# An attention scorer on one core: the last 24 steps in three blocks of eight, and VectorE's share of their weighted sums as halving adds in SBUF

## The chip, the core and the metric

The kernel runs on one core of a Trainium2 chip. The metric is the device time of one execution in microseconds (us). Before the change three runs gave 293.14, 293.26 and 296.01 us; the median is 293.26 us.

## What is computed

For each of B = 512 rows there is a sequence of S = 200 vectors of D = 64 numbers, a target vector and a mask. A small network (256 to 80 to 40 to 1 units, sigmoids between) scores every step against the target. A masked softmax over the 200 scores gives weights, and the output is the weighted sum of the sequence.

```python
tgt = concat([tgt, pos], -1) @ proj_w + proj_b
din = concat([tgt, seq, tgt - seq, tgt * seq], -1)
h = sigmoid(din @ w1 + b1)
h = sigmoid(h @ w2 + b2)
score = (h @ w3 + b3)[..., 0]
score = where(mask == 0, -1e9, score)
attn = softmax(score, -1)
out = einsum('bs,bsd->bd', attn, seq)
```

Everything is fp32.

## The kernel before

The 512 rows lie on 128 partitions, four to a partition (q = 0 to 3). The program is one loop over groups of eight steps (25 groups, index g), and each engine has its own instruction list, written out by hand and tied together with semaphores. Within a group VectorE (DVE in the profile) transposes the sequence (L541), multiplies it with the target (L550) and adds the target's part to the first layer's result (L676, L683). TensorE (PE) does the three layers (L389, L399; L415, L422; L435), and ScalarE (ACT) the nonlinearities (L277, L286, L293).

The stages of a group are shifted against each other: in turn n of the loop, layer 1 works on group n, layer 2 on n - 1, layer 3 on n - 2 and the transposition of the scores and the softmax step on n - 3. There are 25 turns with new groups and three more (n = 25, 26, 27) that only drain.

Layer 3 and what follows it work by blocks of 16 steps: 12 blocks of 16 and a last one of 8, indices c = 0 to 12. After the last group of a block TensorE runs `layer3(c)`, ScalarE copies the scores out (`rows`, L305), TensorE transposes them (L445), and VectorE does `softmax_step(c)`: masked copy, running maximum, subtraction (L659 to L670). ScalarE takes the exponentials (L319). The block's share of the output is then accumulated online: `acc = acc * exp(old max - new max) + sum over steps of e * seq`, with one more column for the sum of the weights.

GpSimd (POOL) does this sum. It multiplies the block with the exponentials into `mix` (L508), copies the exponentials into the extra column (L511), scales `acc` (L512) and halves `mix` by adds until one step is left (L519), then adds it to `acc` (L523). For the last three blocks (`SHARED` = 10, 11, 12) it does only the first rows of each partition (`KEPT` = 2, 1, 1 of the four); VectorE does the others in `share_sum`. VectorE's way differs from GpSimd's: ScalarE writes its exponentials a second time into a PSUM bank (L316, `exp_v`), the product is written with the steps innermost (L637), and one TENSOR_REDUCE (L644) sums it into PSUM (`part_v`); L640 and L646 scale and add to `acc`. `share_sum(10)` stands in turn 25, `share_sum(11)` and `share_sum(12)` behind the loop.

The blocks of the sequence that the sums read are loaded into a ring of two buffers (`seq_sb`, SyncE's queue, L241 and L248). The load of a block waits until the block two before it has been read. Masked scores and shifted scores have two buffers each, the exponentials `E` three.

Of the kernel before, what the change touches and what calls it, by code (L numbers as in the profile page):

```python
# [5 lines left out]
def din_attention_program(nc, r_mask, seq, target, pos_emb, proj_w, proj_b, w1, b1, w2, b2, w3, b3, out):  # L6
# [15 lines left out]
    P = 128  # L22
# [5 lines left out]
    NBLK = -(-S // BLK)  # L28
# [22 lines left out]
    def last_pair(c):  # L51
        return (c * BLK + steps_of(c)) // 2 - 1

    def block_of_last_group(g):
        c = g * 8 // BLK
        return c if 0 <= g < NGRP and 4 * g + 3 == last_pair(c) else None
# [13 lines left out]
    with ctx:  # L70
# [11 lines left out]
        seq_sb = [sb(f"seq_sb{r}", [P, Q, BLK, D]) for r in range(RING)]  # L82
# [52 lines left out]
        mix_v = sb("mix_v", [P, MOST * D * BLK])  # L135
# [12 lines left out]
        s_seq = [sem(f"seq_loaded{r}") for r in range(RING)]  # L148
# [34 lines left out]
        s_exp_v = sem("exp_for_vector_done")  # L183
# [10 lines left out]


        shared_bank = {SHARED: pT, SHARED + 1: pB, SHARED + 2: pL2[0]}

        def exp_v(c):
            w, k = steps_of(c) + 1, Q - KEPT[c]
            return shared_bank[c][:, 0:k * w].rearrange("p (q x) -> p q x", q=k)  # L200

        def part_v(c):
            k = Q - KEPT[c]
            return shared_bank[c][:, 256:256 + k * (D + 1)].rearrange("p (q d) -> p q d", q=k)
# [9 lines left out]
        def _(sp):  # L214
# [527 lines left out]
```

## Time and profile before

| | |
|---|---|
| median of 3 runs | 293.26 us |
| the profiled execution | 293.81 us |
| its span | 292.0 us |
| PE busy | 250.3 us, 86% |
| DVE busy | 235.7 us, 81% |
| POOL busy | 193.7 us, 66% |
| ACT busy | 154.7 us, 53% |
| TensorE's granted clock, mean | 0.972 |

The span runs from the first to the last instruction of the profiled execution; 1.8 us of its time lie around the span. Busy shares are means over the whole span. The loop's body and the drain at its end have different limits, so the end is read by itself, in the timeline.

### The profile page before, as it was taken

How to read it: one execution, taken by the hardware profiler on the slowest of the kernel's cores; microseconds unless marked ns; L12 is line 12 of the kernel's file. 1: busy time of each engine (PE TensorE's matmuls, PEld its weight loads, DVE VectorE, ACT ScalarE, POOL GpSimd, SP SyncE). 2: the span in 40 equal slices, each digit the busy share in tenths (PEclk: the TensorE clock that was granted, in tenths of full speed). 3: DMA queues.
4: the chain of work that ended last, by engine and by line, in shares of the span. 5: the costliest groups of instructions: out<-in, count | busy, mean ns of one | idle time of the engine just before them, and what ended most of it. 6: DMA issues, size and time to landing. Idle time of an engine off the chain costs nothing.

```text
span 292.0 us, 5476 instructions
## 1 busy us (share of the span) xinstructions
PE 250.3 (86%) x2084; PEld 77.9 (27%) x2084; DVE 235.7 (81%) x331; ACT 154.7 (53%) x257; POOL 193.7 (66%) x125
## 2 busy tenths in 40 slices
PE   4659999999999999999999999999999999998100
PEld 2213323222322232323223323322233223222000
DVE  3598999689687886896887868968968799549696
ACT  2003467665666476556755674666566647656100
POOL 2000000009979979979799799797997997987970
PEclk9999999999999999999999999999999999999855
DMA  6989999999799999999999999899898860431200
GB/s 117 167 125 175 162 176 261 214 165 309 126 202 284 179 329 145 161 326 162 270 214 176 323 171 272 201 154 319 130 178 304 133 270 0 136 153 29 114 0 18
DMA packets 216749, 53.68 MB, mean 184 GB/s; under 512 B 209556, under 2 KB 210068, under 8 KB 216724
## 3 DMA queue, kind: packets, MB, share of 16 engines
q1 hardware_dynamic: 211640, 52.70, 82.3%
q10 hardware_dynamic: 5084, 0.64, 1.4%
q8 instruction: 16, 0.26, 0.4%
q14 instruction: 9, 0.07, 0.1%
HBM read 53.20 MB, written 0.13 MB: 183 GB/s over the span
## 4 chain that ended last, share of the span: by engine, by line
DVE 47%; PE 33%; issue 11%; POOL 3%; SPq 2%; DMA 1%; ACT 1%; DVEq 0%; ACTq 0%; POOLq 0%
DVE X L550 15%; PE pA L389 12%; DVE X L541 11%; DVE HidA L676 10%; PE pB L399 8%; PE pA L435 7%; DVE mix_v L637 3%; DVE HidB L683 2%; PE pA L445 2%; PE pL L415 2%; POOL mix L519 2%; POOL mix L508 1%; DVE pB L644 1%; PE pL L422 1%; DMA proj_b<-in_L_rec_proj_b 1%
## 5 line engine op out<-in xcount | busy, mean ns | idle before, releaser
L519 POOL TENSOR_TENSOR mix<-mix 128x260 f32<-128x260 f32 (+5 forms) x51 | 96.9, 1900 | 5.2 <-POOL acc L512 0.5
L277 ACT ACTIVATE HidA<-HidA,VA 128x512 f32<-128x512 f32 x100 | 66.8, 719 | 52.7 <-DVE HidA L676 52.7
L286 ACT ACTIVATE G<-pL,bias 128x512 f32<-128x512 f32 x100 | 60.5, 688 | 47.0 <-PE pL L422 47.0
L508 POOL TENSOR_TENSOR mix<-seq_sb,E 128x4096 f32<-128x4096 f32 (+3 forms) x13 | 77.2, 5941 | 0.4 <-POOL acc L523 0.3
L550 DVE SCALAR_TENSOR_TENSOR X<-pT,P_pair,X 128x512 f32<-128x512 f32 x100 | 69.8, 739 | 0.2
L676 DVE TENSOR_TENSOR HidA<-pA,UA 128x1024 f32<-128x1024 f32 x50 | 59.8, 1196 | 4.6 <-PE pA L389 4.2
L541 DVE STREAM_TRANSPOSE X<-squares 128x1024 f32<-128x1024 f32 x50 | 61.7, 1235 | 0.0
L389 PE MATMUL pA<-X,w_seq 64*64 64x512 f32 x400 | 55.0, 621 | 4.3 <-DVE HidA L676 3.7
L506 POOL MEMSET masked<- 128x64 f32 x11 | 1.7, 152 | 82.5 <-ACT E L319 82.5
L389 PE MATMUL pA<-X,w_sb 64*64 64x512 f32 x400 | 53.7, 608 | 0.0
L399 PE MATMUL pB<-X,wB 128*32 128x512 f32 x400 | 47.8, 596 | 0.0
L415 PE MATMUL pL<-HidA,w2A 64*64 64x512 f32 x400 | 47.6, 590 | 0.0
L683 DVE TENSOR_TENSOR HidB<-pB,UB 128x512 f32<-128x512 f32 x25 | 17.2, 687 | 28.5 <-PE pB L399 28.5
L422 PE MATMUL pL<-HidB,w2B 32*128 32x512 f32 x200 | 28.5, 640 | 0.0
L435 PE MATMUL pA<-G,w3s 128*32 128x512 f32 x200 | 24.1, 599 | 4.8 <-DVE HidA L676 4.8
L389 PEld LDWEIGHTS pA<-X,w_sb 64*64 64x64 f32 x400 | 15.7, 137 | 28.9 <-issue 28.9
L389 PEld LDWEIGHTS pA<-X,w_seq 64*64 64x64 f32 x400 | 12.2, 134 | 40.2 <-issue 26.1
L415 PEld LDWEIGHTS pL<-HidA,w2A 64*64 64x64 f32 x400 | 15.1, 133 | 28.2 <-issue 26.0
L293 ACT ACTIVATE HidB<-HidB,VB 128x512 f32<-128x512 f32 x25 | 18.1, 723 | 7.7 <-DVE HidB L683 7.3
L399 PEld LDWEIGHTS pB<-X,wB 128*32 128x32 f32 x400 | 11.6, 109 | 24.9 <-issue 24.9
L445 PE MATMUL pA<-ident,rows 128*128 128x128 f32 x52 | 8.5, 285 | 6.7 <-DVE HidA L676 4.5
L422 PEld LDWEIGHTS pL<-HidB,w2B 32*128 32x128 f32 x200 | 7.8, 182 | 20.3 <-issue 19.5
(96 smaller groups left out, 106.1 us busy)
## 6 DMA issues: line engine op xcount, KB each, us to landing
squares<-in_L_rec_sequence_emb SPq DMA_DIRECT2D x98, 256.0 KB, 4.7
seq_sb<-in_L_rec_sequence_emb SPq DMA_DIRECT2D x12, 2048.0 KB, 9.9
seq_sb<-in_L_rec_sequence_emb SPq DMA_DIRECT2D x1, 1024.0 KB, 5.1
squares<-in_L_rec_sequence_emb ACTq DMA_DIRECT2D x2, 256.0 KB, 6.1
mask_i<-in_r_mask SPq DMA_DIRECT2D x1, 400.0 KB, 5.5
tgt_sb<-in_L_rec_target_emb SPq DMA_DIRECT2D x1, 128.0 KB, 2.2
out_dram<-result SPq DMA_DIRECT2D x1, 128.0 KB, 2.0
w_sb<-in_L_rec_w ACTq DMA_DIRECT2D x1, 80.0 KB, 3.8
```

The source lines that it names most:

```text
L277: last = nc.scalar.activation(h, h, ACT.Tanh, scale=0.5, bias=VA[:, 4 * u + i:4 * u + i + 1])
L286: nc.scalar.activation(G[p % NG][:, :], pL2[p % 4][:, :], ACT.Tanh, scale=0.5, bias=bias2[:, 0:1])\
L389: last = nc.tensor.matmul(pA[k * HALF:(k + 1) * HALF, i * 512:(i + 1) * 512], w[half, :], x(2 * u + k)[half, :], start=(x is x1), stop=(x ...
L399: last = nc.tensor.matmul(pB[32 * j:32 * j + 32, :], wB_2d(n), x(4 * g + j), start=(n == 0), stop=(n == 1))
L415: nc.tensor.matmul(pL2[2 * k + r][i * HALF:(i + 1) * HALF, :], w2A[half, :], HidA[u % NZA][half, i, :], start=True, stop=False)
L422: last = nc.tensor.matmul(pL2[j][:, :], w2B[quarter, :, :].rearrange("k a m -> k (a m)"), HidB[g % NZB][quarter, :], start=False, stop=True)
L435: last = nc.tensor.matmul(pL3[j * TILE:(j + 1) * TILE, :], w3s[:, k, :], G[p % NG][:, :], start=(k == 0), stop=(k == per - 1))
L508: nc.gpsimd.tensor_tensor(mix[:, 0:k, 0:n, 0:D], seq_sb[c % RING][:, 0:k, 0:n, :], e[:, 0:k, 1:n + 1].unsqueeze(3).to_broadcast([P, k, n, ...
L519: nc.gpsimd.tensor_tensor(mix[:, 0:k, 0:n, :], mix[:, 0:k, 0:n, :], mix[:, 0:k, n:2 * n, :], ALU.add)\
L541: nc.vector.transpose(X1[g % 2][:, 2 * k:2 * k + 2, :], squares[g % SQRING][:, :, 2 * k:2 * k + 2, :].rearrange("p k m d -> p m k d"))\
L550: nc.vector.scalar_tensor_tensor(out=X2[p % NX][:, :], in0=pT[:, :], scalar=P_pair[:, p:p + 1], in1=X1[p // 4 % 2][:, p % 4, :], op0=ALU.a ...
L676: nc.vector.tensor_tensor(HidA[u % NZA][:, :, :], pA[:, :].rearrange("p (i b) -> p i b", i=2), UA[:, :].unsqueeze(1).to_broadcast([P, 2, 5 ...
```

## The change

Blocks are cut anew: 11 blocks of 16 steps and three of 8 (`NFULL` = 11, `SHORT` = 3), c = 0 to 13. Block 10 (steps 160 to 175) stays as it was; steps 176 to 199, which were a block of 16 and one of 8, are blocks 11, 12 and 13. The shared blocks are now 10 to 13, with 2, 1, 1 and 1 rows kept by GpSimd. Each short block has its own `layer3`, `rows`, transposition and softmax step, one turn of the loop after the other (24 to 27), and `share_sum(c)` stands one turn behind the softmax step of c, ahead of that of c + 1.

`share_sum` takes GpSimd's form: the product with the features innermost, a copy of the exponentials into a 65th column, halving adds in `mix_v`, then scaling and adding to `acc`. It reads the exponentials from the same SBUF buffer `E` as GpSimd, and ScalarE writes them once. PSUM has no part in it any longer. Blocks 12 and 13 have sequence buffers of their own, so that their loads wait for nothing; `masked` and `E` have four buffers; two set-up tensors are placed in buffers of `G`.

```diff
-    NBLK = -(-S // BLK)
+    SHORT = 3
+    NFULL = (S - SHORT * 8) // BLK
+    NBLK = NFULL + SHORT
...
-    SHARED = NBLK - 3
-    KEPT = {SHARED: 2, SHARED + 1: 1, SHARED + 2: 1}
+    SHARED = NBLK - 4
+    KEPT = {SHARED: 2, SHARED + 1: 1, SHARED + 2: 1, SHARED + 3: 1}
...
+    def first_step(c):
+        return min(c, NFULL) * BLK + max(c - NFULL, 0) * 8
...
+        def ring(c):
+            return c % RING if c < NBLK - 2 else c - (NBLK - 2) + RING
...
             for c in range((NGRP - 2 - 5) // 2 + 1, NBLK):
-                sp.wait_ge(s_mix, c - RING + 1)
-                if c - RING >= SHARED:
-                    sp.wait_ge(s_part, PART * (c - RING - SHARED) + 1)
+                if c < NBLK - 2:
+                    sp.wait_ge(s_mix, c - RING + 1)
...
                     w = steps_of(c) + 1
-                    k = KEPT.get(c, Q)
-                    if k < Q:
-                        if c == SHARED + 1:
-                            act.wait_ge(s_zb, NGRP)
-                        nc.scalar.activation(exp_v(c), shifted[c % 2][:, k:Q, 0:w], ACT.Exp).then_inc(s_exp_v, 1)
                     if c >= NE:
                         act.wait_ge(s_sum, c - NE + 1)
-                    nc.scalar.activation(E[c % NE][:, 0:k, 0:w], shifted[c % 2][:, 0:k, 0:w], ACT.Exp).then_inc(s_exp, 1)
+                    nc.scalar.activation(E[c % NE][:, :, 0:w], shifted[c % 2][:, :, 0:w], ACT.Exp).then_inc(s_exp, 1)
...
                 n, q0 = steps_of(c), KEPT[c]
                 k = Q - q0
-                done = PART * (c - SHARED)
-                e, part = exp_v(c), part_v(c)
-                prod = mix_v[:, 0:k * D * n].rearrange("p (q d s) -> p q d s", q=k, d=D)
-                dve.wait_ge(s_exp_v, c - SHARED + 1)
-                dve.wait_ge(s_seq[c % RING], 16 * (c // RING + 1))
-                dve.wait_ge(s_sum, SHARED if c == SHARED or KEPT[c - 1] == q0 and c > SHARED + 1 else c)
+                done = parts(c)
+                e = E[c % NE]
+                prod = mix_v[:, 0:k * n * (D + 1)].rearrange("p (q s d) -> p q s d", q=k, s=n)
+                dve.wait_ge(s_exp, c + 1)
+                dve.wait_ge(s_seq[ring(c)], seq_count(c))
                 if done:
                     dve.wait_ge(s_part, done)
-                nc.vector.tensor_tensor(prod.rearrange("p q d s -> p q s d"), seq_sb[c % RING][:, q0:Q, 0:n, :],
-                                        e[:, :, 1:n + 1].unsqueeze(3).to_broadcast([P, k, n, D]), ALU.mult)\
+                nc.vector.tensor_tensor(prod[:, :, :, 0:D], seq_of(c)[:, q0:Q, 0:n, :],
+                                        e[:, q0:Q, 1:n + 1].unsqueeze(3).to_broadcast([P, k, n, D]), ALU.mult)\
                   .then_inc(s_part, 1)
-                nc.vector.tensor_tensor(acc[:, q0:Q, :], acc[:, q0:Q, :], e[:, :, 0:1].to_broadcast([P, k, D + 1]),
+                nc.vector.tensor_copy(prod[:, :, :, D], e[:, q0:Q, 1:n + 1]).then_inc(s_part, 1)
+                done += 2
+                while n > 1:
+                    n //= 2
+                    dve.wait_ge(s_part, done)
+                    nc.vector.tensor_tensor(prod[:, :, 0:n, :], prod[:, :, 0:n, :], prod[:, :, n:2 * n, :], ALU.add)\
+                      .then_inc(s_part, 1)
+                    done += 1
+                if q0 < KEPT.get(c - 1, Q):
+                    dve.wait_ge(s_sum, c)
+                nc.vector.tensor_tensor(acc[:, q0:Q, :], acc[:, q0:Q, :], e[:, q0:Q, 0:1].to_broadcast([P, k, D + 1]),
                                         ALU.mult).then_inc(s_part, 1)
-                nc.vector.tensor_reduce(part[:, :, D:D + 1], e[:, :, 1:n + 1], AX.X, ALU.add).then_inc(s_part, 1)
                 dve.wait_ge(s_part, done + 1)
-                nc.vector.tensor_reduce(part[:, :, 0:D], prod, AX.X, ALU.add).then_inc(s_part, 1)
-                dve.wait_ge(s_part, done + 4)
-                nc.vector.tensor_tensor(acc[:, q0:Q, :], acc[:, q0:Q, :], part, ALU.add).then_inc(s_part, 1)
+                nc.vector.tensor_tensor(acc[:, q0:Q, :], acc[:, q0:Q, :], prod[:, :, 0, :], ALU.add).then_inc(s_part, 1)
...
+                c = block_of_last_group(n - 1 - ST_LAG)
+                if c is not None and c >= SHARED:
+                    share_sum(c)
                 c = block_of_last_group(n - ST_LAG)
                 if c is not None:
                     softmax_step(c)
                 if n + 1 < NGRP:
                     products(2 * n + 3)
-                if n == NGRP:
-                    share_sum(SHARED)
-
-            share_sum(SHARED + 1)
-            share_sum(SHARED + 2)
-            dve.wait_ge(s_part, 3 * PART)
+
+            share_sum(NBLK - 1)
+            dve.wait_ge(s_part, parts(NBLK))
             dve.wait_ge(s_sum, NBLK)
```

VectorE's list at the first shared block, of the kernel before: behind the addition of the last group's target part comes `share_sum(10)` and then the softmax step of block 11. `pT` is a PSUM bank; behind a name stands the form, in brackets the semaphores that the instruction waits for.

```order
L683 TENSOR_TENSOR HidB<-pB,UB 128x512 [waits layer2_done,layer1_last_units_done]
L637 TENSOR_TENSOR mix_v<-seq_sb,pT 128x2x16x64 [waits block_summed,seq_loaded0,exp_for_vector_done]
L640 TENSOR_TENSOR acc<-acc,pT 128x130
L642 TENSOR_REDUCE pT<-pT 128x2
L644 TENSOR_REDUCE pT<-mix_v 128x2x64 [waits vector_sum_step]
L646 TENSOR_TENSOR acc<-acc,pT 128x130 [waits vector_sum_step]
L659 COPY_PREDICATED masked<-mask_i,pA 128x4x16 [waits scores_preset,scores_transposed]
```

The same place in the changed kernel; `mix_v`, `seq_sb`, `E` and `acc` are all in SBUF.

```order
L693 TENSOR_TENSOR HidB<-pB,UB 128x512 [waits layer2_done,layer1_last_units_done]
L640 TENSOR_TENSOR mix_v<-seq_sb,E 128x32x64 [waits seq_loaded0,exp_done]
L643 COPY mix_v<-E 128x32
L648 TENSOR_TENSOR mix_v<-mix_v 128x2x520 [waits vector_sum_step]
L648 TENSOR_TENSOR mix_v<-mix_v 128x2x260 [waits vector_sum_step]
L648 TENSOR_TENSOR mix_v<-mix_v 128x2x130 [waits vector_sum_step]
L648 TENSOR_TENSOR mix_v<-mix_v 128x2x65 [waits vector_sum_step]
L653 TENSOR_TENSOR acc<-acc,E 128x130 [waits block_summed]
L656 TENSOR_TENSOR acc<-acc,mix_v 128x130 [waits vector_sum_step]
L669 COPY_PREDICATED masked<-mask_i,pA 128x4x8 [waits scores_preset,scores_transposed]
```

Five instructions, of which each reads at most one SBUF tensor, have become eight; all but the copy take two SBUF tensors as inputs, and the softmax step behind them is that of a block of eight.

ScalarE's list around turn 24, of the kernel before: the last group's first-layer nonlinearity, then the exponentials of block 10 in two pieces.

```order
L286 ACTIVATE G<-pL,bias 128x512 [waits layer3_done,layer2_done] x4
L277 ACTIVATE HidA<-HidA,VA 128x512 [waits targets_added_first_units]
L277 ACTIVATE HidA<-HidA,VA 128x512
L316 ACTIVATE pT<-shifted 128x34 [waits softmax_step]
L319 ACTIVATE E<-shifted 128x34 [waits block_summed]
L293 ACTIVATE HidB<-HidB,VB 128x512 [waits targets_added_last_units]
```

And of the changed kernel:

```order
L295 ACTIVATE G<-pL,bias 128x512 [waits layer3_done,layer2_done] x4
L314 ACTIVATE rows<-pA,bias 128x512 [waits scores_transposed,layer3_done]
L286 ACTIVATE HidA<-HidA,VA 128x512 [waits targets_added_first_units]
L286 ACTIVATE HidA<-HidA,VA 128x512
L323 ACTIVATE E<-shifted 128x68 [waits block_summed,softmax_step]
L302 ACTIVATE HidB<-HidB,VB 128x512 [waits targets_added_last_units]
```

The `rows` copy of the new block 11 now stands ahead of the exponentials of block 10, which are one piece.

## Rows read from the trace of the kernel before

**Rows 1.** The page, part 4: the chain that ended last, shares of the span.

```profile
DVE 47%; PE 33%; issue 11%; POOL 3%; SPq 2%; DMA 1%; ACT 1%; DVEq 0%; ACTq 0%; POOLq 0%
```

**Rows 2.** Busy time by stretch; columns: stretch, length, busy of each engine, clock, DMA share, GB/s.

```profile
220.00:240.00 20.00, 19.14 (x172) 5.81 (x164) 16.70 (x23) 12.17 (x20) 17.65 (x10) 1.00 0.83 241
264.00:274.00 10.00, 6.16 (x48) 1.82 (x48) 7.71 (x13) 4.94 (x12) 9.40 (x9) 1.00 0.33 105
274.00:284.00 10.00, 0.00 (x0) 0.00 (x0) 9.59 (x6) 0.00 (x0) 8.57 (x16) 0.59 0.00 0
284.00:292.00 8.00, 0.00 (x0) 0.00 (x0) 5.48 (x7) 0.00 (x0) 0.00 (x0) 0.50 0.08 16
```

**Rows 3.** Timeline, 260 to 264 us; columns: start, us, engine, line, operation.

```profile
261.00 1.92 PE L399 MATMUL pB<-X,wB 128*32 128x512 f32 x16
...
262.50 1.34 ACT L277 ACTIVATE HidA<-HidA,VA 128x512 f32<-128x512 f32 x2
...
263.84 0.24 ACT L319 ACTIVATE E<-shifted 128x34 f32<-128x34 f32 x1
...
263.97 3.69 DVE L637 TENSOR_TENSOR mix_v<-seq_sb,pT 128x2048 f32<-128x2048 f32 x1 [0.28 <-ACT pT L316]
```

**Rows 4.** Timeline, 264 to 292 us, without POOL's rows.

```profile
268.42 0.70 ACT L305 ACTIVATE rows<-pA,bias 128x512 f32<-128x512 f32 x1
...
269.82 1.06 PE L435 MATMUL pA<-G,w3s 128*32 128x512 f32 x8
270.11 0.29 DVE L646 TENSOR_TENSOR acc<-acc,pT 128x130 f32<-128x130 f32 x1
...
272.45 0.20 DVE L659 COPY_PREDICATED masked<-mask_i,pA 128x32 f32<-128x32 int32 x1 [1.31 <-PE pA L445]
...
273.15 0.20 ACT L316 ACTIVATE pL<-shifted 128x27 f32<-128x27 f32 x1 [1.26 <-DVE shifted L668]
...
274.24 5.33 DVE L637 TENSOR_TENSOR mix_v<-seq_sb,pB 128x3072 f32<-128x3072 f32 x1 [1.05 <-POOL acc L523]
...
283.67 2.91 DVE L637 TENSOR_TENSOR mix_v<-seq_sb,pL 128x1536 f32<-128x1536 f32 x1
...
288.56 0.36 DVE L646 TENSOR_TENSOR acc<-acc,pL 128x195 f32<-128x195 f32 x1
...
289.16 0.43 DVE L716 TENSOR_TENSOR result<-acc,inv 128x256 f32<-128x256 f32 x1
```

**Rows 5.** Groups of instructions by form on DVE, whole span.

```profile
L676 DVE TENSOR_TENSOR HidA<-pA,UA 128x1024 f32<-128x1024 f32 x50 | 59.8, 1196 | 4.6 <-PE pA L389 4.2
L683 DVE TENSOR_TENSOR HidB<-pB,UB 128x512 f32<-128x512 f32 x25 | 17.2, 687 | 28.5 <-PE pB L399 28.5
...
L640 DVE TENSOR_TENSOR acc<-acc,pL 128x195 f32<-128x195 f32 x1 | 0.3, 348 | 0.0
...
L560 DVE TENSOR_TENSOR w_tgt<-w_sb 64x128 f32<-64x128 f32 x2 | 0.6, 286 | 1.5 <-DMA w_sb<-in_L_rec_w 1.5
```

**Rows 6.** POOL's own rows in the timeline, 264 to 284 us.

```profile
264.24 3.63 POOL L508 TENSOR_TENSOR mix<-seq_sb,E 128x2048 f32<-128x2048 f32 x1
...
273.58 0.46 POOL L523 TENSOR_TENSOR acc<-acc,mix 128x130 f32<-128x130 f32 x1
...
280.17 1.04 POOL L508 TENSOR_TENSOR mix<-seq_sb,E 128x512 f32<-128x512 f32 x1 [0.17 <-POOL acc L523]
...
283.42 0.32 POOL L523 TENSOR_TENSOR acc<-acc,mix 128x65 f32<-128x65 f32 x1
```

**Rows 7.** Groups of instructions by form on POOL, whole span.

```profile
L508 POOL TENSOR_TENSOR mix<-seq_sb,E 128x4096 f32<-128x4096 f32 x10 | 70.7, 7066 | 0.1
L519 POOL TENSOR_TENSOR mix<-mix 128x2080 f32<-128x2080 f32 x10 | 46.4, 4639 | 1.8 <-POOL acc L512 0.5
...
L519 POOL TENSOR_TENSOR mix<-mix 128x65 f32<-128x65 f32 x2 | 0.6, 296 | 0.2
```

**Rows 8.** The page, part 6: the load of a block of sixteen, KB, us to landing.

```profile
seq_sb<-in_L_rec_sequence_emb SPq DMA_DIRECT2D x12, 2048.0 KB, 9.9
```

More of the change, by code:

```diff
@@ L51, in last_pair, with block_of_pair @@
     def last_pair(c):
[L52 removed]
+        return (first_step(c) + steps_of(c)) // 2 - 1
+    def block_of_pair(p):
+        return min(2 * p // BLK, NFULL) + max(2 * p - NFULL * BLK, 0) // 8
     def block_of_last_group(g):
[L55 removed]
+        c = block_of_pair(4 * g)
         return c if 0 <= g < NGRP and 4 * g + 3 == last_pair(c) else None
@@ L80, in sem @@
             return ctx.enter_context(nc.semaphore(name))
-        seq_sb = [sb(f"seq_sb{r}", [P, Q, BLK, D]) for r in range(RING)]
+        seq_sb = [sb(f"seq_sb{r}", [P, Q, BLK, D]) for r in range(RING)] + \
+                 [sb(f"seq_sb{RING + r}", [P, Q, 8, D]) for r in range(2)]
         squares = [sb(f"squares{r}", [P, SQ, 4, TILE]) for r in range(SQRING)]
@@ L128, in din_attention_program @@
         G = [sb(f"G{r}", [P, 512]) for r in range(NG)]
+        tgt_t, P_t = G[NG - 1][0:D, :], G[NG - 2][0:D, 0:S]
         rows = sb("rows", [P, 512])
-        masked = [sb(f"masked{r}", [P, Q, BLK + 1]) for r in range(2)]
+        masked = [sb(f"masked{r}", [P, Q, BLK + 1]) for r in range(NM)]
         shifted = [sb(f"shifted{r}", [P, Q, BLK + 1]) for r in range(2)]
@@ L146, in din_attention_program @@
         pL2 = [ps(f"pL2{i}") for i in range(4)]
-        s_seq = [sem(f"seq_loaded{r}") for r in range(RING)]
+        s_seq = [sem(f"seq_loaded{r}") for r in range(RING + 2)]
         s_sq = [sem(f"squares_loaded{r}") for r in range(SQRING)]
@@ L193, in din_attention_program, with seq_of, seq_count, parts @@
         N_W1, N_SMALL, N_W2, N_LATE = 2, 2, 3, 5
[L196 to L204, printed above, removed]
+        def ring(c):
+            return c % RING if c < NBLK - 2 else c - (NBLK - 2) + RING
+        def seq_of(c):
+            return seq_sb[ring(c)]
+        def seq_count(c):
+            return 16 * (c // RING + 1) if c < NBLK - 2 else 16
+        def parts(c):
+            return sum(4 + steps_of(x).bit_length() - 1 for x in range(SHARED, c))
         block = ctx.enter_context(nc.Block())
@@ L433, in layer3 @@
                     for j in range(NT):
-                        p = c * BLK // 2 + j * per + k
+                        p = first_step(c) // 2 + j * per + k
                         last = nc.tensor.matmul(pL3[j * TILE:(j + 1) * TILE, :], w3s[:, k, :], G[p % NG][:, :],
@@ L490, in _ @@
             pool.wait_ge(s_set, 3)
-            for r in range(2):
+            for r in range(NM):
                 nc.gpsimd.memset(masked[r][:, :, 1:BLK + 1], NEG_INF).then_inc(s_fill, 1)
@@ L504, in _ @@
                     pool.wait_ge(s_sum, c)
-                if c + 2 < NBLK:
-                    nc.gpsimd.memset(masked[c % 2][:, :, 1:BLK + 1], NEG_INF).then_inc(s_fill, 1)
+                if c + NM < NBLK:
+                    nc.gpsimd.memset(masked[c % NM][:, :, 1:BLK + 1], NEG_INF).then_inc(s_fill, 1)
                 k = KEPT.get(c, Q)
-                nc.gpsimd.tensor_tensor(mix[:, 0:k, 0:n, 0:D], seq_sb[c % RING][:, 0:k, 0:n, :],
+                nc.gpsimd.tensor_tensor(mix[:, 0:k, 0:n, 0:D], seq_of(c)[:, 0:k, 0:n, :],
                                         e[:, 0:k, 1:n + 1].unsqueeze(3).to_broadcast([P, k, n, D]), ALU.mult)\
@@ L667, in softmax_step @@
                     dve.wait_ge(s_exp, c - 1)
-                nc.vector.tensor_tensor(shifted[c % 2][:, :, 0:n + 1], masked[c % 2][:, :, 0:n + 1],
+                nc.vector.tensor_tensor(shifted[c % 2][:, :, 0:n + 1], masked[c % NM][:, :, 0:n + 1],
                                         new_max.to_broadcast([P, Q, n + 1]), ALU.subtract).then_inc(s_soft, 1)
-                nc.vector.tensor_copy(masked[(c + 1) % 2][:, :, 0:1], new_max).then_inc(s_soft, 1)
+                nc.vector.tensor_copy(masked[(c + 1) % NM][:, :, 0:1], new_max).then_inc(s_soft, 1)
             def targets_first(u):
```

30 lines of the change are left out of this document (13 added, 17 removed).

## The prediction

> **What bounds the kernel now.** I read the page's chain first, then the stretches, then the timeline of the end, then the groups by form for prices. The chain gives VectorE 47% and TensorE 33% of the span [rows 1], but that is two regimes. In the loop's body TensorE is busy 19.14 of 20.00 us, VectorE 16.70, GpSimd 17.65 [rows 2]: TensorE sets the pace there, and the change leaves blocks 0 to 10 as they are, with the same instructions in the same order. I put nothing on the body. From 274 us on TensorE has no work at all, while VectorE is busy 9.59 of 10.00 us and then 5.48 of 8.00, and GpSimd 8.57 of 10.00 until its share is done [rows 2]. That end is what the change rewrites: from the exponentials of block 10 (263.84 us [rows 3]) to the last division (289.16 + 0.43 = 289.59 us [rows 4]), 25.6 us in which VectorE's sums are the chain.
>
> **The end as it is.** VectorE's share of block 10 runs from 263.97 [rows 3] to 270.11 + 0.29 = 270.40: 6.4 us. Block 11 (three rows of four, 16 steps) runs from 274.24 to 283.67, 9.4 us; block 12 (eight steps) from 283.67 to 288.56 + 0.36 = 288.92, 5.25 us [rows 4]. Together 21.1 us. Between blocks 10 and 11 lie 3.8 us with two short softmax steps and two waits, 1.31 us for TensorE's transposition and 1.05 us for GpSimd's `acc` [rows 4].
>
> **Prices of the new sums if nothing disturbs them.** A contiguous fp32 TENSOR_TENSOR costs 687 ns at 512 elements and 1196 ns at 1024 [rows 5]: 0.18 us fixed and 0.99 ns an element. By that line 195 elements cost 0.37 us (0.348 measured) and 128 cost 0.31 us (0.286 measured; this one, L560, has two SBUF inputs and the set-up has GpSimd idle beside it) [rows 5]. The product of before is dearer, 2.91 us for 1536 elements or 1.89 ns each [rows 4]; it is the only one that writes with a stride (the steps innermost, the features 8 or 16 apart), and the new layout writes 64 in a run, so I price it by the line: 1.70 us for 1536, 2.21 for 2048. The bound on the other side is that the broadcast of the exponentials, not the stride, makes it dear: then it stays at 1.8 ns or so.
> Block 10: product 2.21, copy 0.2, adds of 1040, 520, 260 and 130 elements 1.21 + 0.70 + 0.44 + 0.31, `acc` 0.28 + 0.29: 5.65 us, and as the gaps between chained instructions and the overlaps of unchained ones about cancel, 5.7. A block of eight with three rows: 1.70 + 0.20, adds of 780, 390 and 195 elements 0.95 + 0.57 + 0.37, `acc` 0.35 + 0.36: 4.5 us. All: 5.7 + 3 x 4.5 = 19.2 us, against 21.1: -1.9 us.
>
> **Softmax steps.** Each short block's softmax step now stands directly ahead of its sum: from its first instruction at 272.45 to the exponential's start at 273.15 and 0.20 us on [rows 4], so 0.9 to 0.95 us a time, 2.8 us for three, where before 3.8 us lay between blocks 10 and 11: -1.0 us. The transpositions that they wait for come in time: TensorE starts the last layer 3 at 269.82 us even now [rows 4], and each softmax step only frees the next transposition, which has a sum of 4.5 us to hide in. The 1.31 us of wait goes, and so does the 1.05 us for `acc` if GpSimd isn't slower.
>
> **The front of the end.** In turn 24 TensorE gets `layer3(11)` ahead of the last group's L399: eight records, 1.06 us [rows 4], from 261.00 to about 262.1 [rows 3]. ScalarE copies `rows` (0.70 us [rows 4]) at 262.50, where its next nonlinearity stood [rows 3], so this and the exponentials of block 10 move by 0.6 us; one exponential over all rows saves the second piece, but the first piece was what VectorE waited for. VectorE's first product starts at 264.6 instead of 263.97: +0.65 us. L399 and what hangs on it come 0.9 us later, which ends in the drain's slack.
> Queues: SyncE's last load of before waited for VectorE's product of block 10; now the loads of blocks 12 and 13 follow that of block 11 at once. Block 11's load waits for GpSimd's product of block 9, behind which come adds of which the first alone takes 4.6 us [rows 7], all before 264.24 [rows 6]; so it starts ahead of 259 us. A load of 2 MB lands in 9.9 us [rows 8]; the 3 MB of the three loads are there by 274, and block 12 is read at 276. No gain, no loss, unless the loads were late, which no row says. More buffers for `masked` and `E`, the set-up tensors in `G` and two more memsets at the start: nothing, GpSimd idles there.
> Sum without a collision: -1.9 - 1.0 + 0.65 = -2.3 us.
>
> **What the trace of before doesn't show: both engines reading two SBUF tensors at once.** In this kernel VectorE's instructions in the loop and in `share_sum` have one SBUF input at most, the other lies in PSUM (`pT`, `pA`, `pB`, `part`). After the change 25 of the 29 instructions of the four shares read two SBUF tensors, and in all this time GpSimd does the same. No row prices that. GpSimd's own rows say that its time goes by what it must read: its product, where one input is a repeated element, costs 7066 ns for 4096, 1.73 ns each, its add with two full streams 4639 ns for 2080, 2.23 ns each [rows 7]. So a contest over the way to SBUF is possible, and I bound it.
> - Below: nothing, each engine keeps its times: -2.3 us in all. Nothing in this hardware's rows lets either engine gain by it.
> - Above: each instruction of one waits for a whole instruction of the other, in turns. GpSimd's share of block 10 takes 264.24 to 274.04, 9.8 us, of an eight-step block 280.17 to 283.74, 3.6 us [rows 6]. VectorE then waits for all of it but the last add of each block (0.46 and 0.32 us [rows 6]): 9.3 + 3 x 3.25 = 19.1 us more, and 0.3 us for GpSimd's last add ahead of the division. -2.3 + 19.4 = +17 us.
> - Between: in turns, but only while data stream. A POOL add of 65 elements costs 296 ns [rows 7], so some 0.2 us of each instruction is fixed, and VectorE has 0.18 us of its own; these can lie beside each other. Block 10: 9.8 us less 8 x 0.25 (fixed parts and gaps) less 8 x 0.2 of VectorE's gives 6.2 us; an eight-step block gives about 1 us. -2.3 + 9.2 = +7 us.
> I take turns, midway between the last two: +12 us, because the two engines' instructions are of the same kind, always queued at the same moments (both start at the same exponentials, block for block), and the rows show a fixed part on both but not that it hides. Then block 10's share ends at about 277, not 270, the later softmax steps come after it, and each later block takes 7 us instead of 5.4.
> The Trainium skill speaks against the change here: "SBUF — State Buffer", section "Who interferes with whom", says that a VectorE instruction with two SBUF inputs contends with a GpSimd instruction that reads SBUF, that the pair of ports is locked for a whole instruction, and that the second to come blocks fully. No run or row here shows it yet. By that rule the sum is the upper one, near +17 us; by the durations in the trace taken alone it is -2.3 us.
>
> The profiled execution took 293.81 us, 0.55 above the median of 293.26. From its own rows the sum gives 305.8; from the median 305.3. I say 305.5.
>
> **Rivals.**
> 1. No collision. The end shortens as planned: -2.3 us, 291 to 291.5 us. For it: L560's two SBUF inputs cost no more than the line [rows 5]. Against: GpSimd was idle there. This is the case on the other side, not slower; it holds if VectorE's 2048-element product beside GpSimd's takes 2.2 us and GpSimd's L508 stays at 3.6. It decides as long as the collision costs less than 2.3 us.
> 2. The two share the way to SBUF access by access: both go on, each slower while both stream. VectorE streams some 14 of its 19.2 us, GpSimd works beside it for nearly all; at half again the time that is +7, less where GpSimd is done early: +5 net of the -2.3 at most, 295 to 300 us, middle 297. For it: nothing but that it is milder. Against: nothing either.
> 3. No collision, but the product keeps its old price: 0.8 ns more on 2048 + 3 x 1536 elements, +5.3 us: 296.3 us. Against: GpSimd's and VectorE's other broadcasts run at full rate (L640, 195 elements in 348 ns, reads one repeated element per row) [rows 5].
> That it doesn't do what it says is no rival; the order of the instructions shows it.
>
> **How the numbers follow.** Turns 0.60 (300 to 311, middle 305.5), no collision 0.20, shared access 0.15, dear product 0.05. A measurement of this kernel can tell about 1%, 2.9 us, from no change. Slower by over 1% (above 296.2): 0.60, 0.15 of rival 2 nearly whole, half of rival 3: 0.77. Rival 1 at -0.8% lies mostly within 1%: same 0.15, faster 0.08. The range must reach rival 1 to leave out no more than 2 in 10: 290.7 to 310.5; the forecast's own range is 300 to 311.
>
> **What would show it.** Right: VectorE's product of block 10 and GpSimd's first product no longer start together and run side by side; the starts of the two engines' instructions alternate; rows of POOL or DVE at the same size as before are longer or have idle time ahead of them; `share_sum(10)` takes 11 to 15 us and the span ends near 304. Wrong: the new VectorE adds stand at 1.2, 0.7 and 0.44 us in a row beside GpSimd's unchanged adds, and the last division is near 287. A first product of `share_sum(10)` that starts far from 264.6 us would overturn the step on the body or the one on the front.

## The result and the profile after

The changed kernel takes 303.34 us (median of 4 runs, 302.26 to 304.59), the kernel before in the same comparison 294.5 us (4 runs, 293.14 to 296.01). The ratio is 1.030 with a 95% interval of 1.0215 to 1.0385: slower by 3%, 8.8 us. Forecast were 305.5 us, in a range of 290.7 to 310.5, and slower with a chance of 0.77.

The profiled execution took 304.59 us, span 302.8. VectorE is still 81% busy; the chain's shares hardly moved from those of before [rows 1]. The page, part 4:

```profile
DVE 48%; PE 33%; issue 11%; SPq 2%; POOL 2%; ACT 1%; DMA 1%; DVEq 0%; POOLq 0%; ACTq 0%
```

So the shares say nothing of the cause. The stretches answer to [rows 2]; columns as there.

```profile
220.00:240.00 20.00, 19.14 (x172) 5.96 (x168) 16.70 (x23) 12.40 (x22) 17.67 (x10) 1.00 0.86 250
...
274.00:284.00 10.00, 2.95 (x12) 0.91 (x12) 9.53 (x13) 0.92 (x2) 9.33 (x9) 0.50 0.00 0
284.00:294.00 10.00, 1.08 (x4) 0.71 (x4) 9.21 (x20) 0.47 (x2) 7.91 (x12) 0.50 0.00 0
294.00:303.00 9.00, 0.00 (x0) 0.00 (x0) 5.93 (x9) 0.00 (x0) 5.27 (x7) 0.50 0.07 15
```

The body is the same to a hundredth (19.14 and 16.70 us in 20). The end is longer, and both VectorE and GpSimd count as busy nearly all through it. An engine that is held up inside an instruction is busy by this count; only the lengths of its instructions tell. VectorE's rows of the end (start, us, engine, line, operation), to set beside [rows 3 and 4]:

```profile
263.05 0.23 DVE L669 COPY_PREDICATED masked<-mask_i,pA 128x64 f32<-128x64 int32 x1 [0.75 <-PE pA L449]
...
266.54 2.29 DVE L640 TENSOR_TENSOR mix_v<-seq_sb,E 128x2048 f32<-128x2048 f32 x1
...
268.75 3.61 DVE L643 COPY mix_v<-E 128x32 f32<-128x32 f32 x1
...
272.40 5.87 DVE L648 TENSOR_TENSOR mix_v<-mix_v 128x1040 f32<-128x1040 f32 x4
...
279.05 0.19 DVE L669 COPY_PREDICATED masked<-mask_i,pA 128x32 f32<-128x32 int32 x1
...
280.00 1.76 DVE L640 TENSOR_TENSOR mix_v<-seq_sb,E 128x1536 f32<-128x1536 f32 x1 [0.23 <-ACT E L323]
...
281.68 0.19 DVE L643 COPY mix_v<-E 128x24 f32<-128x24 f32 x1
281.90 3.12 DVE L648 TENSOR_TENSOR mix_v<-mix_v 128x780 f32<-128x780 f32 x3
...
285.83 0.20 DVE L669 COPY_PREDICATED masked<-mask_i,pA 128x32 f32<-128x32 int32 x1
...
299.96 0.42 DVE L726 TENSOR_TENSOR result<-acc,inv 128x256 f32<-128x256 f32 x1
```

A copy of 32 elements takes 3.61 us. Four halving adds that cost 2.77 us without GpSimd (shown below) take 5.87. GpSimd's rows beside them, to set beside [rows 6]:

```profile
266.59 5.73 POOL L512 TENSOR_TENSOR mix<-seq_sb,E 128x2048 f32<-128x2048 f32 x1 [2.49 <-ACT E L323]
...
272.43 1.48 POOL L516 TENSOR_TENSOR acc<-acc,E 128x130 f32<-128x130 f32 x1
...
280.18 2.49 POOL L512 TENSOR_TENSOR mix<-seq_sb,E 128x512 f32<-128x512 f32 x1 [0.17 <-POOL acc L527]
...
282.61 0.94 POOL L515 COPY mix<-E 128x8 f32<-128x8 f32 x1
```

Read together they are turns. VectorE's product starts at 266.54, GpSimd's 0.05 us later; GpSimd's lasts 5.73 us instead of 3.63, which is 2.1 us more: VectorE's 2.29 us less some 0.2 us, near the 0.18 us that the prediction's line gave as the fixed part. VectorE's own product keeps the 2.29 us that it takes without GpSimd (shown below), so the one that came first lost nothing. VectorE's copy is issued at 268.75 and ends at 272.36, 0.04 us after GpSimd's product. In a short block VectorE's product comes first again and GpSimd's takes 2.49 us instead of 1.04; then the first add waits for that. The copy between them does not wait there (0.19 us); the last section comes back to it.

The measure for all that follows is the stretch from VectorE's first product to the end of the last division. Before it is 25.62 us (263.97 to 289.59), after it 33.84 us (266.54 to 300.38): +8.2. From the softmax step of block 10 to the first product it is 3.49 us after, and before 261.11 to 263.97, 2.86 us: +0.63. Together they are 8.85 us, as is the difference of the medians (8.84). The remaining 1.94 us of the span are not of the change. Here the two profiled executions differ at the start, shown by the first L399 of the kernel before, in the timeline (and below it the start of that softmax step):

```profile
27.19 1.93 PE L399 MATMUL pB<-X,wB 128*32 128x512 f32 x16
...
261.11 0.23 DVE L659 COPY_PREDICATED masked<-mask_i,pA 128x64 f32<-128x64 int32 x1 [0.75 <-PE pA L445]
```

and its counterpart after:

```profile
27.50 3.57 PE L403 MATMUL pB<-X,wB 128*32 128x512 f32 x16
```

The same sixteen records took nearly twice as long in one execution as in the other, and all that follows is 1.94 us later. The profile doesn't show why: the granted clock of this stretch reads 1.00 in both. In a later run whose rows are as long (3.64 us, the kernel before with another layout) it reads 0.50, TensorE's level of 1.2 GHz. The times of both kernels fall into two groups 2 us apart (293.14 and 293.26 against 295.74 and 296.01; 302.26 and 302.32 against 304.35 and 304.59), so the stretch is the steadier measure.

### The profile page after: what moved, and what is told of

It is laid out like the page before. It is cut to its first block, busy times and chain, and to the rows that moved or that the text cites. A ratio compares the mean times of both kernels' runs of the same rounds, so it can differ in the third digit from the quotient of the medians.

```text
span 302.8 us, 5516 instructions
## 1 busy us (share of the span) xinstructions
PE 254.6 (84%) x2088; PEld 79.6 (26%) x2088; DVE 245.2 (81%) x349; ACT 155.5 (51%) x256; POOL 205.9 (68%) x132
## 4 chain that ended last, share of the span: by engine, by line
DVE 48%; PE 33%; issue 11%; SPq 2%; POOL 2%; ACT 1%; DMA 1%; DVEq 0%; POOLq 0%; ACTq 0%
DVE X L554 14%; PE pA L393 12%; DVE X L545 11%; DVE HidA L686 9%; PE pB L403 9%; PE pA L439 7%; DVE mix_v L648 4%; DVE HidB L693 2%; PE pA L449 2%; DVE mix_v L640 2%; PE pL L419 2%; DVE mix_v L643 1%; PE pL L426 1%; DMA proj_b<-in_L_rec_proj_b 1%; DVE masked L669 1%
## 5 line engine op out<-in xcount | busy, mean ns | idle before, releaser
L523 POOL TENSOR_TENSOR mix<-mix 128x260 f32<-128x260 f32 (+5 forms) x53 | 98.0, 1850 | 5.1
L512 POOL TENSOR_TENSOR mix<-seq_sb,E 128x4096 f32<-128x4096 f32 (+2 forms) x14 | 84.1, 6008 | 4.2 <-ACT E L323 4.0
L403 PE MATMUL pB<-X,wB 128*32 128x512 f32 x400 | 49.5, 613 | 0.0
L693 DVE TENSOR_TENSOR HidB<-pB,UB 128x512 f32<-128x512 f32 x25 | 17.2, 687 | 31.1 <-PE pB L403 31.1
L439 PE MATMUL pA<-G,w3s 128*32 128x512 f32 x200 | 25.2, 617 | 4.8 <-DVE HidA L686 4.8
L449 PE MATMUL pA<-ident,rows 128*128 128x128 f32 x56 | 10.0, 306 | 18.0 <-DVE masked L680 13.5
L648 DVE TENSOR_TENSOR mix_v<-mix_v 128x780 f32<-128x780 f32 (+6 forms) x13 | 14.9, 1148 | 0.4
```

Of the source, the lines that this page charges most:

```text
L403: last = nc.tensor.matmul(pB[32 * j:32 * j + 32, :], wB_2d(n), x(4 * g + j), start=(n == 0), stop=(n == 1))
L439: last = nc.tensor.matmul(pL3[j * TILE:(j + 1) * TILE, :], w3s[:, k, :], G[p % NG][:, :], start=(k == 0), stop=(k == per - 1))
L512: nc.gpsimd.tensor_tensor(mix[:, 0:k, 0:n, 0:D], seq_of(c)[:, 0:k, 0:n, :], e[:, 0:k, 1:n + 1].unsqueeze(3).to_broadcast([P, k, n, D]), AL ...
L523: nc.gpsimd.tensor_tensor(mix[:, 0:k, 0:n, :], mix[:, 0:k, 0:n, :], mix[:, 0:k, n:2 * n, :], ALU.add)\
```

## The experiments

All are compared with the kernel before on the same chip; the ratio is to it, with its 95% interval.

### GpSimd's sums left out

```diff
+                if c >= SHARED:
+                    nc.gpsimd.memset(mix[:, 0:1, 0:1, 0:1], 0.0).then_inc(s_mix, 1)
+                    nc.gpsimd.memset(mix[:, 1:2, 0:1, 0:1], 0.0).then_inc(s_sum, 1)
+                    continue
```

> GpSimd leaves its sums of blocks 10 to 13 out (two tiny memsets a block keep the signals), so the output lacks its rows' last 40 steps; VectorE's instructions are those of the changed kernel. If GpSimd's reads hold VectorE's two-SBUF instructions up, block 10's share falls from 12.6 to 5.7 us and each short one from 5.9 to 4.5, first product to end of the last division from 33.8 to about 22.8 us, time near 292.3 us. If the short blocks or the order of the new list cost the time (rival), the shares keep their lengths and the time stays above 300 us.

Measured: 291.47 us, ratio 0.9928 (0.9894 to 0.9961); the stretch is 264.58 to 287.20, 22.62 us. VectorE's rows:

```profile
264.58 2.29 DVE L644 TENSOR_TENSOR mix_v<-seq_sb,E 128x2048 f32<-128x2048 f32 x1
266.79 0.19 DVE L647 COPY mix_v<-E 128x32 f32<-128x32 f32 x1
267.01 2.77 DVE L652 TENSOR_TENSOR mix_v<-mix_v 128x1040 f32<-128x1040 f32 x4
...
270.23 0.20 DVE L673 COPY_PREDICATED masked<-mask_i,pA 128x32 f32<-128x32 int32 x1
...
271.19 1.76 DVE L644 TENSOR_TENSOR mix_v<-seq_sb,E 128x1536 f32<-128x1536 f32 x1 [0.23 <-ACT E L323]
...
275.64 0.20 DVE L673 COPY_PREDICATED masked<-mask_i,pA 128x32 f32<-128x32 int32 x1
```

The same instructions, in the same order. Block 10's share takes 5.65 us (264.58 to 270.23) against 12.51 after, a short one 4.45 against 5.83 (280.00 to 285.83). 6.9 + 3 x 1.4 = 11.0 us are thus GpSimd's presence, and 33.84 - 22.62 = 11.2 says the same, with 0.3 us of waiting for GpSimd's last add. Short blocks, order and prices are as planned. The rival falls. This kernel leaves work out, so its time is no gain.

### The cut into short blocks alone

```diff
-                prod = mix_v[:, 0:k * n * (D + 1)].rearrange("p (q s d) -> p q s d", q=k, s=n)
-                dve.wait_ge(s_exp, c + 1)
...
+                e, part = exp_v(c), part_v(c)
+                prod = mix_v[:, 0:k * D * n].rearrange("p (q d s) -> p q d s", q=k, d=D)
+                dve.wait_ge(s_exp_v, c - SHARED + 1)
...
+                nc.vector.tensor_reduce(part[:, :, 0:D], prod, AX.X, ALU.add).then_inc(s_part, 1)
```

> Three short blocks in the changed kernel's order, but VectorE's sums in the form of before (exponentials and partial sums in PSUM, product with the steps innermost, TENSOR_REDUCE): the cut into short blocks alone. Turns on SBUF as the cause: no collision, shares of 6.4 and 3 x 5.25 us plus 0.65 at the front, 0.9 us over the kernel before: about 294.4 us. If the short blocks themselves cost the time (rival): over 299 us.

Measured: 295.31 us, ratio 1.004 (1.0003 to 1.0077); the stretch is 264.68 to 290.55, 25.87 us. GpSimd's rows have the lengths of before (product 3.62 and 1.04 us). Three blocks of eight instead of sixteen and eight cost 0.3 us here and 0.6 at the front, no more. (The medians differ by 1.8 us; five of its ten runs fell into the later of the two groups, against seven of nineteen of the kernel before.)

### The halving adds alone, in the long blocks

```diff
-                nc.vector.tensor_reduce(part[:, :, 0:D], prod, AX.X, ALU.add).then_inc(s_part, 1)
...
+                while n > 1:
+                    n //= 2
+                    dve.wait_ge(s_part, done)
+                    nc.vector.tensor_tensor(prod[:, :, 0:n, :], prod[:, :, 0:n, :], prod[:, :, n:2 * n, :], ALU.add)\
+                      .then_inc(s_part, 1)
+                    done += 1
```

> The kernel before with its blocks of 16, 16, 8, but VectorE's share as halving adds that read E and mix_v in SBUF: the form alone. Turns: block 10's share 12.6 us, block 11's 7.8 + about 3.5, block 12's 5.9, against 21.1 in all before, less the waits for TensorE and for acc that this hides: 7 us over before, about 300.5 us. Without a collision (rival: the short blocks are the cause): 3 us below before, 290.5 us.

Measured: 301.37 us, ratio 1.026 (1.0206 to 1.0313); the stretch is 265.15 to 296.79, 31.64 us. The form alone, without short blocks, brings most of the loss. The same 3.6 us copy is there. In block 12 GpSimd came first, and VectorE's product of 1536 elements is the one that waits (L634, 2.48 us instead of 1.76); in block 11 GpSimd's copy of 16 elements does, 3.34 us instead of 0.21:

```profile
267.36 3.62 DVE L637 COPY mix_v<-E 128x32 f32<-128x32 f32 x1
...
280.36 3.54 DVE L634 TENSOR_TENSOR mix_v<-seq_sb,E 128x3072 f32<-128x3072 f32 x1
...
290.24 2.48 DVE L634 TENSOR_TENSOR mix_v<-seq_sb,E 128x1536 f32<-128x1536 f32 x1
```

```profile
280.63 3.34 POOL L509 COPY mix<-E 128x16 f32<-128x16 f32 x1
...
290.06 1.04 POOL L506 TENSOR_TENSOR mix<-seq_sb,E 128x512 f32<-128x512 f32 x1 [0.17 <-POOL acc L521]
```

So among the instructions that collide, who is blocked is a matter of who comes second.

### The exponentials back in PSUM, the adds left in SBUF

```diff
-                e = E[c % NE]
+                e = exp_v(c)
...
-                dve.wait_ge(s_exp, c + 1)
+                dve.wait_ge(s_exp_v, c - SHARED + 1)
```

> Changed kernel, but ScalarE writes VectorE's exponentials to PSUM as before, and product, column copy and scaling read them there; only the halving adds and the last add still have two SBUF inputs. Whole-instruction turns: GpSimd's products return to 3.63 and 1.04 us, the copy of block 10 from 3.6 to 0.2 us, the first add of block 10 waits for the end of GpSimd's product, the rest still alternates: 4 us less, about 299 us. If the two share the way access by access (rival): rows grow only in proportion to the overlap, the first add of block 10 starts right behind the copy (2.5 us after the product's start), not at 3.7 us.

Measured: 298.16 us, ratio 1.0146 (1.0082 to 1.0211); the stretch is 263.95 to 292.78, 28.83 us, 5.0 less than after.

```profile
263.95 2.29 DVE L656 TENSOR_TENSOR mix_v<-seq_sb,pT 128x2048 f32<-128x2048 f32 x1
266.15 0.21 DVE L659 COPY mix_v<-pT 128x32 f32<-128x32 f32 x1
```

```profile
L664 DVE TENSOR_TENSOR mix_v<-mix_v 128x1040 f32<-128x1040 f32 x1 | 2.5, 2465 | 0.0
```

```profile
264.14 3.62 POOL L528 TENSOR_TENSOR mix<-seq_sb,E 128x2048 f32<-128x2048 f32 x1 [2.58 <-ACT E L339]
267.71 1.25 POOL L531 COPY mix<-E 128x32 f32<-128x32 f32 x1
```

With one SBUF input VectorE's product and GpSimd's run side by side, both at their own lengths. The first add, which has two, starts at 266.40 and takes 2.465 us instead of 1.24: it ends 1.1 us behind GpSimd's product (267.76), that is at its own price from there, less some 0.13 us. GpSimd's copy behind the product then waits for the add (1.25 us instead of 0.24). That is the whole-instruction turn: for 1.36 us the add overlaps a product that stays at 3.62 us, and a sharing of single accesses would have made the product longer and the add's wait shorter. The sign that the expectation named, the start of the add, tells nothing: a waiting instruction starts early and is long.

Nor is the cause that both engines read the same tensor. The two products both read `seq_sb` and don't collide; the add reads only `mix_v`, which GpSimd never reads, and it does.

Of the 5.0 us, 2.2 are in block 10: GpSimd's product, no longer held by VectorE's, ends 2.0 us sooner after VectorE's first start (3.81 us against 5.78), and what VectorE has waiting behind it goes on sooner.

### The copy as a reduce

```diff
-                nc.vector.tensor_copy(prod[:, :, :, D], e[:, q0:Q, 1:n + 1]).then_inc(s_part, 1)
+                nc.vector.tensor_reduce(prod[:, :, :, D:D + 1], e[:, q0:Q, 1:n + 1].unsqueeze(3), AX.X, ALU.add).then_inc(s_part, 1)
```

> Changed kernel; the copy into the 65th column is a TENSOR_REDUCE over one element, so it has one SBUF input and is no copy. If a plain SBUF-to-SBUF copy itself takes part in the turns: the 3.6 us of block 10's copy go to 0.2, but the first halving add then waits for the same GpSimd product, so the share stays at 12.5 us and the time at 303. If the copy only stood behind something that any VectorE instruction would stand behind (rival): the reduce takes 3.6 us too.

Measured: 302.03 us, ratio 1.0293 (1.0239 to 1.0346); the stretch is 263.88 to 297.66, 33.78 us, as after.

```profile
266.10 0.20 DVE L643 TENSOR_REDUCE mix_v<-E 128x32 f32<-128x32 f32 x1
266.33 9.21 DVE L648 TENSOR_TENSOR mix_v<-mix_v 128x1040 f32<-128x1040 f32 x4
```

The reduce of block 10 doesn't wait, though its input and its output are the same SBUF tensors: this copy of 32 elements takes part in the turns, a TENSOR_REDUCE doesn't. But the 3.4 us only moved, from the copy to the first add (9.21 us for the four against 5.87): both would have waited for the same product. A row's length is no gain that its removal brings.

### GpSimd only writes

```diff
+                if c >= SHARED:
+                    m = 4 if n == BLK else 2
+                    nc.gpsimd.memset(mix[:, 0:m, :, :], 0.0).then_inc(s_mix, 1)
+                    pool.wait_ge(s_mix, c + 1)
+                    for r in range(2):
+                        nc.gpsimd.memset(mix[:, 0:m // 2, :, :], 0.0).then_inc(s_tree, 1)
...
```

> Changed kernel; GpSimd's sums of blocks 10 to 13 are replaced by memsets that only write SBUF (the output lacks its rows' last 40 steps): one of 4160 elements and two of 2080 in block 10, half of that in a short one, some 3.5 + 2 x 1.8 us in block 10 by the memset of 260 elements. If the contest is for reading: VectorE's product and adds keep 2.29, 1.24, 0.70, 0.43 us beside them, and the time is that of the run without GpSimd's sums, 291.5 us, unless the copy alone waits (up to 3.5 us more). If it is for SBUF in general (rival): the adds wait as in the changed kernel, block 10's share takes over 9 us, 297 us or more.

Measured: 292.64 us, ratio 0.9957 (0.9925 to 0.9989); the stretch is 263.99 to 287.86, 23.87 us.

```profile
263.99 2.29 DVE L650 TENSOR_TENSOR mix_v<-seq_sb,E 128x2048 f32<-128x2048 f32 x1
266.20 1.43 DVE L653 COPY mix_v<-E 128x32 f32<-128x32 f32 x1
267.67 2.77 DVE L658 TENSOR_TENSOR mix_v<-mix_v 128x1040 f32<-128x1040 f32 x4
```

```profile
264.02 3.56 POOL L513 MEMSET mix<- 128x4160 f32 x1 [2.48 <-ACT E L323]
267.64 3.72 POOL L516 MEMSET mix<- 128x2080 f32 x2
```

Product and adds, all with two SBUF inputs, keep their lengths beside memsets that run from 264.02 to 271.36. Only the copy waits, 1.2 us, for the end of the first memset at 267.58, and the stretch is longer than without GpSimd's sums by just that. So the contest of the two-input instructions is for reading, and the copy's is for writing too.

### Does the layout of the product matter

The third rival of the prediction. Two kernels whose `share_sum` has no instruction with two SBUF inputs, the short one of above and the kernel before, with the product written in runs of 64 and the reduce reading it with a stride:

```diff
-                prod = mix_v[:, 0:k * D * n].rearrange("p (q d s) -> p q d s", q=k, d=D)
+                prod = mix_v[:, 0:k * D * n].rearrange("p (q s d) -> p q s d", q=k, d=D)
...
-                nc.vector.tensor_reduce(part[:, :, 0:D], prod, AX.X, ALU.add).then_inc(s_part, 1)
+                nc.vector.tensor_reduce(part[:, :, 0:D], prod.rearrange("p q s d -> p q d s"), AX.X, ALU.add).then_inc(s_part, 1)
```

> Short blocks, exponentials and partial sums in PSUM, no halving adds: as the run of the short blocks alone, but VectorE writes its product in runs of 64 and TENSOR_REDUCE reads it with a stride. If only strided writing is dear: product 2.29 and 1.76 us instead of 3.69 and 2.93, reduce as before (2.29, 1.76): 4.9 us less than that run, about 290 us, and the first kernel here below the one before. If strided reading is as dear as strided writing (rival): the reduce rises to 3.7 and 2.9 us and the time stays at 295.

> The kernel before with the same exchange alone (contiguous product, strided reduce). If only strided writing is dear: block 10's share 1.4 us shorter, which the wait for GpSimd's acc swallows, block 11's 2.0 and block 12's 1.2 us shorter: 3.2 us below before, about 290.3 us. If strided reading costs the same (rival): as before.

Measured: 294.62 us, ratio 1.0011 (0.9976 to 1.0047), for the short blocks, and 293.65 us, ratio 1.0007 (0.9975 to 1.0038), for the kernel before. The groups by form on VectorE, of the short one:

```profile
L656 DVE TENSOR_TENSOR mix_v<-seq_sb,pB 128x1536 f32<-128x1536 f32 x1 | 1.8, 1754 | 0.2 <-ACT pB L336 0.2
...
L661 DVE TENSOR_REDUCE pB<-mix_v 128x192 f32<-128x1536 f32 x1 | 2.8, 2801 | 0.0
```

The product falls from 2.9 to 1.75 us, as priced, and the reduce rises from 1.75 to 2.80. So the rival of both expectations held: strided reading is as dear as strided writing, some 1.8 ns an element, and the exchange is about one for one. What the halving adds win, when nothing holds them, is that neither side has a stride: a short share of 4.45 us without GpSimd's sums, against 5.32 us with the strided product.

### A form without two SBUF inputs, and GpSimd's idle time used

A tensor in PSUM is no SBUF input. In the short blocks the product's lower half is written to SBUF and its upper half to PSUM, and each add takes one operand from either; block 10 keeps the form of before.

```diff
+                    low = mix_v[:, 0:k * 4 * (D + 1)].rearrange("p (q s d) -> p q s d", q=k, s=4)
+                    up = pL2all[:, 0:k * 4 * (D + 1)].rearrange("p (q s d) -> p q s d", q=k, s=4)
...
+                    nc.vector.tensor_tensor(low[:, :, 0:2, :], low[:, :, 0:2, :], up[:, :, 0:2, :], ALU.add).then_inc(s_part, 1)
+                    nc.vector.tensor_tensor(up[:, :, 2:4, :], low[:, :, 2:4, :], up[:, :, 2:4, :], ALU.add).then_inc(s_part, 1)
```

> Short blocks; block 10 in the form of before, blocks 11 to 13 by halving adds of which each reads one half from SBUF and the other from PSUM (the product's upper half is written there), so no instruction of VectorE has two SBUF inputs. If two SBUF inputs are the cause, the halving adds run beside GpSimd at their own price: 4.9 us a short block against 5.3 in the run of the short blocks alone, GpSimd's rows unchanged at 1.04 and 0.20 us, 294.1 us. If halving adds as such collide (rival): 5.8 us or more a block, over 296 us.

Measured: 293.31 us, ratio 0.997 (0.9937 to 1.0003); the stretch is 264.14 to 288.18, 24.04 us.

```profile
271.51 0.95 DVE L671 TENSOR_TENSOR mix_v<-seq_sb,pB 128x768 f32<-128x768 f32 x1 [0.19 <-ACT pB L338]
...
273.53 0.56 DVE L678 TENSOR_TENSOR mix_v<-mix_v,pL 128x390 f32<-128x390 f32 x1
274.01 0.56 DVE L679 TENSOR_TENSOR pL<-mix_v,pL 128x390 f32<-128x390 f32 x1
...
276.21 0.20 DVE L704 COPY_PREDICATED masked<-mask_i,pA 128x32 f32<-128x32 int32 x1
```

And GpSimd's product meanwhile:

```profile
274.29 1.04 POOL L530 TENSOR_TENSOR mix<-seq_sb,E 128x512 f32<-128x512 f32 x1 [0.17 <-POOL acc L545]
```

A short share takes 4.7 us (271.51 to 276.21) with four instructions more than the changed kernel's, which takes 5.83, and GpSimd's product keeps its 1.04 us. Halving adds as such don't collide. The time is the same as before the change, within 2%.

Then GpSimd's idle time. GpSimd takes a second row of block 12, and waits for VectorE's sum of block 11 before it scales `acc`.

```diff
-    KEPT = {SHARED: 2, SHARED + 1: 1, SHARED + 2: 1, SHARED + 3: 1}
+    KEPT = {SHARED: 2, SHARED + 1: 1, SHARED + 2: 2, SHARED + 3: 1}
```

> The same, and GpSimd keeps two rows of block 12 instead of one, since it idled 2.5 us after that block. Without a collision VectorE's block 12 falls from 4.9 to 3.6 us: 292.8 us, 0.2% below the kernel before. If GpSimd's longer sum of block 12 holds the last block's acc up (rival): no gain over the run before it, 294 us.

Measured: 293.23 us, ratio 0.9959 (0.9925 to 0.9992); the stretch is 266.94 to 290.92, 23.98 us. VectorE is done at 289.18, 22.24 us behind the first product where the run before it had 23.38 (1.1 us less), and then waits for GpSimd:

```profile
290.29 0.18 DVE L761 RECIPROCAL inv<-acc 128x4 f32<-128x4 f32 x1 [1.11 <-POOL acc L547]
```

Both readings were half right: VectorE gained nearly what was expected, and GpSimd's last `acc` took nearly all of it back. These two kernels can't be told from each other (293.31 and 293.23 us, stretches of 24.04 and 23.98). Against the kernel before, 293.75 us here, the last one is 0.2% lower by the medians and 0.4% by the ratio, and its interval leaves 1 out only barely: the same within 2%. The form without GpSimd's sums, with work left out, is 0.7% under, so even without a collision this end had little to give.

## Why the prediction was right

Point by point, by its own steps.

- **The body.** Untouched, as said; 19.14 of 20 us.
- **The front.** 0.65 us forecast, 0.63 measured. The exponentials moved by 0.64 us, as said. But the 0.9 us by which L399 and what hangs on it come later (0.86 measured) did not end in slack: it brought VectorE's own addition L693 up to 0.03 us ahead of the exponentials' end. Any later, and the front would have followed it instead.

```profile
265.79 0.69 DVE L693 TENSOR_TENSOR HidB<-pB,UB 128x512 f32<-128x512 f32 x1 [1.91 <-PE pB L403]
```

```profile
266.23 0.28 ACT L323 ACTIVATE E<-shifted 128x68 f32<-128x68 f32 x1
```

- **Prices without a collision.** -2.3 us forecast. Without GpSimd's sums the stretch is 3.0 us shorter than before, plus 0.63 at the front: -2.4 (the medians differ by 2.0). Products 2.29 and 1.76 us against 2.21 and 1.70 forecast, short shares 4.45 against 4.5.
- **Both engines reading two SBUF tensors.** The mechanism taken, turns, is what the rows show, and it decides the sign. Its size was too large: 14.3 us (12 + 2.3), measured 11.2, so the change cost 8.8 us where +12 was forecast. The total of 305.5 looks closer to 303.34 than that, because the forecast was added to 293.26 and the kernel before took 294.5 in the comparison. The mis-sized term is the midway value: the bounds of block 10 were 6.2 and 9.3 us, and it was 6.9; those of a short block 1 and 3.25, and it was 1.4. Both lie near the lower bound, "in turns, but only while data stream". The prediction also disagreed with itself: block 10's share ending at 277 instead of about 270, and later blocks of 7 us instead of 5.4, are 6.7 + 3 x 1.6 = 11.5 us of waits, not 14.3. Measured were 12.5 us for the share and 6.8 for a later block, so its picture was right and the step from it to the sum was not. The rows show two reasons for the size. An instruction that has waited ends at its own price behind the other's end less about 0.15 us, so fixed parts do hide: the copy ends 0.04 us behind GpSimd's product, though by itself it takes 0.19. And the waiting falls on both: in a short block GpSimd's product waits 1.45 us for VectorE's, which costs little since GpSimd has time there (it is idle 0.74 us ahead of the next block). In block 10 the same wait comes back, as VectorE's copy waits for that product.
- **No collision (rival 1)** is refuted by GpSimd's product row (5.73 us, where it asked for 3.6) and by the run without GpSimd. **Shared access (rival 2)** by GpSimd's product, 2.1 us longer beside a product of VectorE's that lost nothing, and by the first add in the run with the exponentials in PSUM. **Dear product (rival 3)** by 1.75 us for 1536 elements; its ground, that broadcasts run at full rate, held.
- **What would show it**: block 10's share was to take 11 to 15 us and took 12.5; the two products did start together, against what I wrote, and GpSimd's was stretched instead. That sentence was wrong: a blocked instruction shows a start and a long duration, not a late start.

The Trainium skill's "SBUF — State Buffer", section "Who interferes with whom", states that the port pair shared by VectorE and GpSimd is an exclusive lock for a whole instruction, that two SBUF inputs contend only with GpSimd's reads, that copies can contend and TENSOR_REDUCE doesn't. This case's traces agree with each: 2.465 us for an add behind a product, 2.29 us for a product beside a memset, 1.43 us for a copy of 32 elements beside it and 0.20 us for a reduce beside a product. Adding up whole instructions by that rule gave +17 us, and 8.8 were measured: fixed parts overlap, and part of the waits fall on the engine with slack.

## What to carry to other kernels

When VectorE and GpSimd work side by side, count the SBUF inputs of each VectorE instruction. One input in SBUF and one in PSUM ran free here; two in SBUF took turns with each GpSimd instruction that reads SBUF, and so did a copy of 32 elements from SBUF to SBUF, which waited for a writing one too. A longer-looking form (a reduce over a strided product, stretch 25.9 us, or adds with one half in PSUM, 24.0) beats a cheaper one that has to take turns (33.8). And before shortening a row that looks absurd, ask what the next instruction would wait for: the 3.6 us copy was worth nothing.

## What was not expected of the hardware

- A copy of 32 elements from SBUF to SBUF waited even beside a memset, which reads nothing: 1.43 us instead of 0.19. A two-input product of 2048 elements beside the same memset kept 2.29 us.
- Reading with a stride of 256 bytes costs TENSOR_REDUCE what writing with a stride of 32 or 64 bytes costs TENSOR_TENSOR: 2.80 and 2.91 us for 1536 elements, against 1.75 without a stride. The Trainium skill's "Advanced Engine Details and Errata", section "Memory Cachelines", asks for two hits on a 16-byte line for full speed; the traces agree for reads and writes alike, at 1.8 to 1.9 ns an element instead of 1.1. All strides here are 32 bytes or more, so no run shows the size of the line.
- The copy behind VectorE's own product, without a wait between them, did not wait in the short blocks (24 elements, 281.68, 0.19 us), though GpSimd's product ran until 282.67, while in block 10 the copy of 32 elements waited 3.4 us. Either it went ahead of GpSimd's product or it takes no part in the turns. The rows don't tell: with the TENSOR_REDUCE in its place GpSimd's product takes the same 2.49 us. The two copies differ in shape too (three rows of 8 steps against two of 16). What decides it was not tried.
